# Half of the MLP's gating moved from VectorE to GpSimd, and every engine's order written anew

## The chip, the cores and the metric

The kernel runs on one core of a Trainium2 chip. The metric is the device time of one execution in microseconds (us); the times here are medians of several executions. The engines are PE (TensorE), DVE (VectorE), ACT (ScalarE), POOL (GpSimd) and SP (SyncE, which here only issues DMAs). Each runs its own queue of instructions strictly in order and waits on semaphores for the others.

## The reference, cut to what matters

The program is a transformer block followed by a cross-attention layer, on 4 batches of 1024 rows and 256 channels, all in float32. Four stages follow each other for each row:

```
A  h = LN(x)*(1+s)+b;  x += gate * windowed_self_attention(h)     # windows of 128, 16 heads
B  h = LN(x)*(1+s)+b;  x += gate * topk_cross_attention(h, ctx)   # the 16 largest of 77 scores
C  h = LN(x)*(1+s)+b;  u = h @ w_m1 + b_m1                        # 256 -> 2 x 1024
   a, b = u[..., :1024], u[..., 1024:]
   x += gate * ((silu(a) * b) @ w_m2 + b_m2)                      # 1024 -> 256
D  h = LN(x)*scale+bias;  out = x + cross_attention(h, ctx) @ Wp + bp
```

The change concerns `silu(a) * b` in stage C.

## The kernel before, in words

The 4096 rows are 32 tiles of 128 rows. Every tile passes the four stages, and different tiles are in different stages at the same time: while tile t is normalised for stage A, tile t-1 or so is in B, tile t-4 in C, tile t-6 in D. Each engine has a list of steps (`fill`, then `body(i)` for i = 8 to 31, then `drain`), written out in full: a step such as `up(t, j)` is a few instructions behind its waits. `run(step, i, lag, ...)` in a body calls the step for tile i - lag. The order within these lists is the whole schedule; nothing is chosen while the kernel runs.

PSUM has eight banks of 512 words. Banks 0 to 3 hold the wide score matrices of A, B and D in turn; banks 4 to 7 are shared by all other results, as the table `BANK` says (A's output and the up group 2 are both in bank 5, for instance). `claim` makes PE wait until the last holder of a bank has been read.

Stage C works on the transposed normalised tile `HT["C"]`. The hidden width 1024 is eight groups of 128, one to a partition. For group j, `up(t, j)` (L2336) makes four float32 matmuls, recorded as eight, into bank `C.up{j}`: columns 0 to 127 are a, columns 128 to 255 are b. `silu(t, j)` (L1039, ACT) writes silu(a + bias) to `SA`, and `hidden(t, j)` (L1666, DVE) writes (b + bias) * SA to `G`, of which there are two copies, and frees the bank. `down(t, half)` (L2348, PE) multiplies four groups of `G` with `w_m2` into bank `C.dn0`; half 0 takes groups 0 to 3, half 1 groups 4 to 7. `gated` (DVE) and `add_residual` (POOL) then make the input of stage D.

In `body`, PE's order around this is: transpose_h D, three transpose_p B, scores_t, up 0, project_q D, weigh_values B and A, scores D, up 1, project_o B, up 2 to 4, project_o A, up 5 to 7, down 0, project_k, down 1, project_q A, transpose_h C and B, weigh_values D, scores_a, project_q B, project_o D, project_v, transpose_max, scores B. `maxima_a` (L1522, DVE) reads the scores of scores_a, and transpose_max (L2250) turns what it wrote.

DVE also does the selection of the 16 largest scores (`select`, four units of four heads, steps 0 to 3: MAX8, MATCH_REPLACE8, MAX8, MATCH_REPLACE8), `keep_chosen` (L1583), the statistics of the layer norms, residual adds and transposes. POOL does the reciprocal roots of the norms (`reciprocal_root`, L613), subtractions of maxima (`less_max`, `top_less_max`), normalisations, bias adds and `add_residual` (L703). SP's order places the DMAs: turning the tile and the stage-D weights through DRAM, loads of x and of weights, stores of the output.

Of the kernel before, what the change touches and what calls it, by code (L numbers as in the profile page):

```python
# [7 lines left out]
ALU = mybir.AluOpType  # L8
# [4 lines left out]
P = 128  # L13
# [62 lines left out]
G_COPIES = 2  # L76
TURNED = {"A": range(1, 32)}
WEIGHTS_TURNED = {"D": range(1, 26)}

def block_kernel(nc, a, out):  # L80
    ctx = ExitStack()
    with ctx:
# [87 lines left out]
        with ExitStack() as early:  # L170
# [43 lines left out]
        ld = {n: sem(f"ld_{n}") for n in ("cond", "small", "mod_a", "mod", "gate", "rows", "qkv", "so",  # L214
                                          "b", "kv_b", "kv_d", "up", "down", "ctx")}
# [33 lines left out]
        u_ps, sa_ok, g_ok = sem("u_ps"), sem("sa_ok"), sem("g_ok")  # L249
# [90 lines left out]
        def _(sp):  # L340
# [110 lines left out]
            def fill():  # L451
                write_tables()
                write_turned(1, "A")
                read_tables(0)
                read_turned(1, "A")
                load_next_x(2)
                read_tables(1)
                load_next_x(3)
                write_turned(2, "A")
                read_turned(2, "A")  # L460
                load_context_weights()
                load_mlp_weights(0)
                write_turned(3, "A")
                load_next_x(4)
                read_tables(2)
                read_turned(3, "A")
                write_flat("B")
                load_mlp_weights(1)
                read_flat("B")
                write_turned(4, "A")  # L470
                load_next_x(5)
                read_turned(4, "A")
                load_mlp_weights(2)
                load_next_x(6)
                write_flat("D")
                write_turned(5, "A")
                read_turned(5, "A")
                read_flat("D")
                write_turned(6, "A")
                load_next_x(7)  # L480
                read_turned(6, "A")

            def body(i):
                run(write_weights, i, 8, "D", 0)
                run(write_weights, i, 8, "D", 1)
                run(load_next_x, i, 0)
                run(store_y, i, 9)
                run(read_weights, i, 8, "D", 0)
                run(read_weights, i, 8, "D", 1)
                run(write_turned, i, 1, "A")  # L490
                run(read_turned, i, 1, "A")

            def drain():
                store_y(TILES - 9)
                write_weights(TILES - 8, "D", 0)
                write_weights(TILES - 8, "D", 1)
                read_weights(TILES - 8, "D", 0)
                read_weights(TILES - 8, "D", 1)
                write_turned(TILES - 1, "A")
                read_turned(TILES - 1, "A")  # L500
                write_weights(TILES - 7, "D", 0)
                write_weights(TILES - 7, "D", 1)
                read_weights(TILES - 7, "D", 0)
                read_weights(TILES - 7, "D", 1)
                store_y(TILES - 8)
# [17 lines left out]
            load_weights(rows[:], a["rows"].partition_broadcast(BATCH).rearrange("p a n c -> p (a n) c"), "rows")  # L523
# [6 lines left out]
            load_weights(w_kv["B"][:], a["w_kv"], "kv_b")  # L530
# [12 lines left out]
        def _(pool):  # L543
# [38 lines left out]
            def set_up_value_masks():  # L582
                pool.wait_ge(ld["ctx"], 16 * 3)
# [118 lines left out]

            def add_residual(t):  # L703
# [9 lines left out]
            def fill():  # L713
                reciprocal_root(0, "A")
                reciprocal_root(1, "A")
                set_up_masks()
                add_bias(0, "A")
                add_bias(1, "A")
                set_up_value_masks()
# [3 lines left out]
                set_up_context_rstd()  # L723
                reciprocal_root(0, "B")
                add_bias(2, "A")
                reciprocal_root(3, "A")
                add_bias(0, "B")
                less_max(0, "B", 0)
                divide_a(1)
                add_bias(1, "B")  # L730
                less_max(0, "B", 1)
                reciprocal_root(4, "A")
                reciprocal_root(1, "B")
                top_less_max(0)
                normalise_weights(0, "B", 0)
                add_bias(3, "A")
                normalise_weights(0, "B", 1)
                set_up_values("B")
                less_max(1, "B", 0)
                divide_a(2)  # L740
                top_less_max(1)
                less_max(1, "B", 1)
                reciprocal_root(2, "B")
                reciprocal_root(0, "C")
                normalise_weights(1, "B", 0)
                normalise_weights(1, "B", 1)
                reciprocal_root(5, "A")
                less_max(2, "B", 0)
                add_bias(4, "A")
                less_max(2, "B", 1)  # L750
                add_bias(0, "C")
                divide_a(3)
                set_up_keys("D")
                reciprocal_root(3, "B")
                reciprocal_root(1, "C")
                top_less_max(2)
                add_residual(0)
                normalise_weights(2, "B", 0)
                normalise_weights(2, "B", 1)
                reciprocal_root(0, "D")  # L760
                set_up_values("D")
                clear_pads()
                less_max(3, "B", 0)
                divide_a(4)
                add_bias(1, "C")
                reciprocal_root(6, "A")
                add_bias(2, "B")
                less_max(0, "D", 0)
                top_less_max(3)
                less_max(3, "B", 1)  # L770
                less_max(0, "D", 1)
                add_bias(5, "A")
                reciprocal_root(4, "B")
                add_bias(2, "C")
                reciprocal_root(2, "C")
                add_residual(1)
                normalise_weights(3, "B", 0)
# [3 lines left out]
                add_bias(3, "B")  # L781
                fold_sums(0)
                normalise_weights(0, "D", 0)
                less_max(4, "B", 0)
                divide_a(5)
                reciprocal_root(7, "A")
                normalise_weights(0, "D", 1)
                less_max(1, "D", 0)
                add_bias(1, "D")
                reciprocal_root(3, "C")  # L790
                reciprocal_root(5, "B")
                add_bias(6, "A")
                less_max(1, "D", 1)
                top_less_max(4)
                less_max(4, "B", 1)
                add_residual(2)
                add_bias(7, "A")
                reciprocal_root(2, "D")
                add_bias(4, "B")

            def body(i):
                run(normalise_weights, i, 4, "B", 0)
                run(normalise_weights, i, 4, "B", 1)
                run(fold_sums, i, 7)
                run(reciprocal_root, i, 0, "A")
                run(less_max, i, 3, "B", 0)
                run(add_bias, i, 5, "C")
                run(add_bias, i, 6, "D")
                run(normalise_weights, i, 7, "D", 0)
                run(divide_a, i, 2)  # L810
                run(normalise_weights, i, 7, "D", 1)
                run(less_max, i, 3, "B", 1)
                run(less_max, i, 6, "D", 0)
                run(reciprocal_root, i, 4, "C")
                run(reciprocal_root, i, 2, "B")
                run(add_bias, i, 0, "A")
                run(less_max, i, 6, "D", 1)
                run(top_less_max, i, 3)
                run(add_bias, i, 3, "B")
                run(add_residual, i, 5)  # L820
                run(reciprocal_root, i, 5, "D")

            def drain():
                normalise_weights(TILES - 4, "B", 0)
                normalise_weights(TILES - 4, "B", 1)
                fold_sums(TILES - 7)
                add_bias(TILES - 3, "B")
                normalise_weights(TILES - 7, "D", 0)
                add_bias(TILES - 6, "D")
                divide_a(TILES - 2)  # L830
                add_bias(TILES - 5, "C")
                normalise_weights(TILES - 7, "D", 1)
                reciprocal_root(TILES - 4, "C")
                less_max(TILES - 3, "B", 0)
                reciprocal_root(TILES - 2, "B")
                add_bias(TILES - 4, "C")
                less_max(TILES - 3, "B", 1)
                top_less_max(TILES - 3)
                less_max(TILES - 6, "D", 0)
                less_max(TILES - 6, "D", 1)  # L840
                add_residual(TILES - 5)
# [3 lines left out]
                fold_sums(TILES - 6)  # L845
                less_max(TILES - 2, "B", 0)
                add_bias(TILES - 5, "D")
                less_max(TILES - 2, "B", 1)
                add_bias(TILES - 2, "B")
                normalise_weights(TILES - 6, "D", 0)  # L850
                divide_a(TILES - 1)
                normalise_weights(TILES - 6, "D", 1)
# [55 lines left out]
        def _(act):  # L908
# [1835 lines left out]
```

## Time and profile before

| | us |
|---|---|
| median of 3 runs | 971.22 (970.75 to 972.36) |
| profiled execution | 972.71 |
| its span, first to last instruction | 970.9 |

| engine | busy us | share | instructions |
|---|---|---|---|
| PE | 922.6 | 95% | 10500 |
| DVE | 867.8 | 89% | 4318 |
| ACT | 744.8 | 77% | 1604 |
| POOL | 701.7 | 72% | 1099 |

The profile is one execution, recorded instruction by instruction. A busy share counts the time in which an engine has an instruction in it, and neighbouring instructions overlap: the next one starts before the last has left. So what an instruction costs its engine is better read from one start to the next than from its duration. A releaser is what ended an idle time.

### The profile page before, as it was taken

Reading aid. Unit: us, or ns where it says so; the run is one execution under the profiler, and the core shown is the slowest. Engines: PE = TensorE matmul, PEld = TensorE weight load, DVE = VectorE, ACT = ScalarE, POOL = GpSimd, SP = SyncE. Lnnn points to the kernel's source line nnn. Section 1 sums busy time; section 2 is a strip of 40 time slices with the busy share of each in tenths; the row PEclk is TensorE's granted clock in tenths of the full one; section 3 lists DMA queues with packets and bytes.
Section 4 is the critical chain, followed back from the end, with each engine's and each line's share of the span. In section 5 each row is a group of like instructions: output and inputs, shape, how many; then the busy total and the mean of one; then the engine's idle time right before and its main releaser. Section 6 shows DMA issues by size and latency. Waiting matters only on the chain. (4 is left out here: it accounts for less than half of the span.)

```text
span 970.9 us, 32585 instructions
## 1 busy us (share of the span) xinstructions
PE 922.6 (95%) x10500; PEld 803.2 (83%) x10500; DVE 867.8 (89%) x4318; ACT 744.8 (77%) x1604; POOL 701.7 (72%) x1099
## 2 busy tenths in 40 slices
PE   6777999999999999999999999999999999999996
PEld 4555888888889888888889888888889888888784
DVE  3587999999999999999999999999999999998643
ACT  2464778888878888888888887888888888887773
POOL 1525587887777888887777777887777887777652
PEclk9997999999999999999999999999999999999999
DMA  8464310123333333223333333223333332220000
GB/s 296 139 132 109 37 17 10 31 65 78 72 72 78 78 65 57 62 64 78 72 72 79 77 54 65 62 67 78 72 73 78 78 67 52 50 63 7 7 6 18
DMA packets 210555, 66.44 MB, mean 68 GB/s; under 512 B 188520, under 2 KB 200961, under 8 KB 209746
## 3 DMA queue, kind: packets, MB, share of 16 engines
q1 hardware_dynamic: 210386, 64.35, 30.2%
q8 instruction: 86, 1.41, 0.6%
q14 instruction: 83, 0.68, 0.2%
HBM read 39.02 MB, written 25.30 MB: 66 GB/s over the span
## 5 line engine op out<-in xcount | busy, mean ns | idle before, releaser
L2344 PE MATMUL ps<-hT_C,w_m_sb 128*128 128x128 f32 x2048 | 257.4, 278 | 1.3 <-DVE hidden_C L1674 0.8
L2344 PEld LDWEIGHTS ps<-hT_C,w_m_sb 128*128 128x128 f32 x2048 | 243.8, 192 | 14.5 <-issue 8.3
L1043 ACT ACTIVATE silu_C<-ps,cols_sb 128x128 f32<-128x128 f32 x256 | 93.4, 366 | 117.3 <-PE ps L2344 106.3
L2355 PE MATMUL ps<-w_m_sb,hidden_C 128*128 128x256 f32 x512 | 120.8, 380 | 0.0
L1580 DVE MATCH_REPLACE8 scores_left_B<-mx_B,scores_left_B 128x77 f32<-128x77 f32 x512 | 108.9, 229 | 0.0
L1576 DVE MATCH_REPLACE8 scores_left_B<-mx_B,scores_B 128x77 f32<-128x77 f32 x512 | 108.4, 226 | 0.0
L2355 PEld LDWEIGHTS ps<-w_m_sb,hidden_C 128*128 128x128 f32 x512 | 92.7, 190 | 10.3 <-DVE hidden_C L1674 0.2
L666 POOL TENSOR_TENSOR scores_D<-scores_D,mx_D 128x616 f32<-128x616 f32 x62 | 75.9, 1227 | 25.2 <-DVE mx_D L1647 25.2
L1674 DVE SCALAR_TENSOR_TENSOR hidden_C<-ps,cols_sb,silu_C 128x128 f32<-128x128 f32 x256 | 84.1, 339 | 8.8 <-ACT silu_C L1043 8.7
L701 POOL TENSOR_TENSOR p_B<-p_B,rc_B 128x616 f32<-128x616 f32 x64 | 76.9, 1218 | 17.4 <-DVE p_B L1588 13.0
L701 POOL TENSOR_TENSOR p_D<-scores_D,rc_D 128x616 f32<-128x616 f32 x63 | 77.0, 1225 | 12.0 <-DVE rc_D L1625 6.3
L661 POOL TENSOR_TENSOR p_B<-scores_B,mx_B 128x616 f32<-128x616 f32 x64 | 78.5, 1227 | 8.9 <-DVE mx_B L1574 8.9
L1574 DVE MAX8 mx_B<-scores_B 128x8 f32<-128x77 f32 x512 | 80.1, 227 | 2.6 <-ACT scores_B L1014 2.2
L1578 DVE MAX8 mx_B<-scores_left_B 128x8 f32<-128x77 f32 x512 | 81.4, 225 | 0.0
L1528 DVE TENSOR_REDUCE mx_A<-ps 128x8 f32<-128x1024 f32 x64 | 75.1, 1216 | 3.1 <-PE ps L2246 3.1
L992 ACT ACTIVATE pT_A<-ps 128x1024 f32<-128x1024 f32 x64 | 63.7, 1068 | 2.5 <-PE ps L2263 2.1
L1588 DVE SCALAR_TENSOR_TENSOR p_B<-scores_left_B,p_B 128x616 f32<-128x616 f32 x64 | 51.2, 800 | 1.1 <-ACT p_B L1020 1.1
L976 ACT ACTIVATE kblk_A<-ps,kb_bias,mask_sb 128x128 f32<-128x128 f32 x128 | 47.6, 450 | 3.8 <-PE ps L2226 3.8
L2301 PE MATMUL ps<-ident_sb,p_B 128*128 128x128 f32 x320 | 44.9, 279 | 5.2 <-POOL p_B L701 4.3
L1036 ACT COPY pT_B<-ps 128x512 f32<-128x512 f32 (+1 forms) x96 | 47.7, 540 | 1.6 <-PE ps L2301 1.5
L1647 DVE TENSOR_REDUCE mx_D<-scores_D 128x8 f32<-128x616 f32 x62 | 47.8, 773 | 0.4 <-ACT scores_D L1014 0.4
L1014 ACT COPY scores_B<-ps 128x616 f32<-128x616 f32 x64 | 40.1, 679 | 9.5 <-PE ps L2287 9.1
(188 smaller groups left out, 2434.8 us busy)
## 6 DMA issues: line engine op xcount, KB each, us to landing
p_turned_D<-p_blocks_D SPq DMA_DIRECT2D x200, 80.0 KB, 2.4
pT_D<-p_turned_D SPq DMA_DIRECT2D x50, 320.0 KB, 3.6
xn_turned_A<-xn_blocks_A SPq DMA_DIRECT2D x124, 32.0 KB, 2.0
xn_A<-xn_turned_A SPq DMA_DIRECT2D x31, 128.0 KB, 2.1
x_A<-in_x SPq DMA_DIRECT2D x28, 128.0 KB, 2.3
out<-y_D SPq DMA_DIRECT2D x28, 128.0 KB, 2.0
w_m_sb<-in_w_m SPq DMA_DIRECT2D x3, 1024.0 KB, 5.2
w_mod_sb<-in_w_mod SPq DMA_DIRECT2D x2, 1024.0 KB, 10.0
```

Of the source, the lines that this page charges most:

```text
L661: g.tensor_tensor(where, S["B"][:, heads, :], MXB[:, heads, 0:1].to_broadcast([P, HH, LC]), ALU.subtract).then_inc(sm_ok["B"], 1)
L666: g.tensor_tensor(where, where, MXD[:, heads, :].to_broadcast([P, HH, LC]), ALU.subtract).then_inc(sm_ok["D"], 1)
L701: g.tensor_tensor(where, src, rc, ALU.mult).then_inc(n_ok[s], 1)
L1043: sc.activation(SA[:, j, :], bank(f"C.up{j}")[:, 0:P], ACT.Silu, bias=col("bm1_a", j)).then_inc(sa_ok, 1)
L1528: v.tensor_reduce(MXA[:, :, :, c], wide[:, :, c * 2 * P:(c + 1) * 2 * P].rearrange("p g (j k) -> p g j k", j=2), AX.X, ALU.max).then_inc(m ...
L1574: ins = v.max(MXB[:, h, 0:8], S["B"][:, h, :])
L1576: ins = v.match_replace(R[:, h, :], MXB[:, h, 0:8], S["B"][:, h, :], LOW)
L1578: ins = v.max(MXB[:, h, 8:16], R[:, h, :])
L1580: ins = v.match_replace(R[:, h, :], MXB[:, h, 8:16], R[:, h, :], LOW)
L1674: v.scalar_tensor_tensor(out=G[:, t % G_COPIES, j, :], in0=bank(f"C.up{j}")[:, P:2 * P], scalar=col("bm1_b", j), in1=SA[:, j, :], op0=ALU. ...
L2344: ins = mm(bank(f"C.up{j}")[:, half * P:(half + 1) * P], w_m1[:, k, m:m + P], HT["C"][:, t % HT_COPIES["C"], k, :], start=(k == 0), stop=( ...
L2355: ins = mm(bank("C.dn0")[:, 0:CH], G[:, t % G_COPIES, j, :], w_m2[:, j, :], start=(j == 0), stop=(j == HJ - 1))
```

## The change

`DIRECT = HJ // 2` is 4. Groups 0 to 3 are gated by DVE as before. For groups 4 to 7 `silu` also copies b + bias from the bank into `G` on ACT, which frees the bank, and one POOL instruction a tile multiplies `SA` into `G` in place.

```diff
+DIRECT = HJ // 2
+            def multiply_rest(t):                       # POOL
+                pool.wait_ge(sa_ok, HJ * t + HJ)
+                pool.wait_ge(ub_ok, (HJ - DIRECT) * (t + 1))
+                rest = G[:, t % G_COPIES, DIRECT:, :]
+                g.tensor_tensor(rest, SA[:, DIRECT:, :], rest, ALU.mult).then_inc(gp_ok, 1)
             def silu(t, j):                             # ACT
                 act.wait_ge(u_ps, HJ * t + j + 1)
                 if not first(t):
-                    act.wait_ge(g_ok, HJ * (t - 1) + j + 1)
+                    if j < DIRECT:
+                        act.wait_ge(g_ok, DIRECT * (t - 1) + j + 1)
+                    else:
+                        act.wait_ge(gp_ok, t)
                 sc.activation(SA[:, j, :], bank(f"C.up{j}")[:, 0:P], ACT.Silu, bias=col("bm1_a", j)).then_inc(sa_ok, 1)
+                if j >= DIRECT:
...
+                    if t >= G_COPIES:
+                        act.wait_ge(y_ps["C"], t + 1 - G_COPIES)
+                    sc.activation(G[:, t % G_COPIES, j, :], bank(f"C.up{j}")[:, P:2 * P], ACT.Identity, bias=col("bm1_b", j)).then_inc(ub_ok, 1)
             def up(t, j):                               # PE
-                claim(BANK[f"C.up{j}"], (g_ok, HJ * t + j + 1))
+                if j < DIRECT:
+                    claim(BANK[f"C.up{j}"], (g_ok, DIRECT * t + j + 1))
+                else:
+                    claim(BANK[f"C.up{j}"], (ub_ok, (HJ - DIRECT) * t + j - DIRECT + 1))
             def down(t, half):                          # PE
-                pe.wait_ge(g_ok, HJ * t + (half + 1) * HJ // 2)
+                if half == 0:
+                    pe.wait_ge(g_ok, DIRECT * (t + 1))
+                else:
+                    pe.wait_ge(gp_ok, t + 1)
```

Two semaphores of the fill are merged into others (`rows` into `gate`, `kv_b` into `ctx`), since two new ones are needed. All lists are made anew, steady body, fill and drain, on PE, DVE, ACT, POOL and SP. The steady bodies, where they differ (steps named with their lag):

```diff
 PE    ... weigh_values_a, scores D, up 1,
-      project_o B, up 2, up 3, up 4, project_o A, up 5, up 6, up 7, down 0, project_k, down 1,
-      project_q A, transpose_h C, transpose_h B, weigh_values D, scores_a, project_q B, project_o D, project_v,
+      up 2, up 3, project_o B, project_o A, up 4, up 5, up 6, up 7, down 0, project_k, project_q A, down 1,
+      transpose_h B, scores_a, weigh_values D, project_q B, transpose_h C, project_v, project_o D,
       transpose_max, scores B
 POOL
+      fold_sums 7, normalise D 7 (0, 1), root A 0, divide_a 2, less_max B 3 (0), add_bias D 7, add_bias B 4,
+      less_max B 3 (1), add_bias A 0, add_bias C 5, less_max D 6 (0), top_less_max 3, root B 2,
+      multiply_rest 5, less_max D 6 (1), root C 4, add_residual 5, normalise B 3 (0), root D 5, normalise B 3 (1)
 ACT
+      output_t B, silu 0, modulate A, silu 1 to 3, normalise A, copy_scores D (0, 1), silu 4 to 7,
+      exponentials B (0), normalise B, key_blocks, queries A, top_exponentials, modulate B, normalise C,
+      exponentials B (1), output_t D, exponentials D (0), queries B, modulate C, normalise D, values,
+      exponentials D (1), copy_scores B (0, 1), weights_t B (0, 1, 2), modulate D, exponentials_a (0, 1), queries D
 SP
-      write_weights 0, 1, load x, store y, read_weights 0, 1, write_turned, read_turned
+      read_turned, write_weights 0, 1, read_weights 1, store y, read_weights 0, write_turned, load x
```

On DVE the four remaining `hidden` steps stand after the output turns of stage A, each beside selection steps; `maxima_a` follows `gated`, turn_input, row_sums B and statistics D, and the second keep_chosen now comes after it. In the fill, SP's `load_mlp_weights(1)` and `(2)` move behind `write_flat("D")`, `read_flat("D")` and `read_tables(2)`; PE makes `project_k(0)`, the gates and the bias before `project_q(0, "A")`.

## Rows read from the trace of the kernel before

**Rows 1.** The page's busy time: engine, busy us, share of the span, instructions.
```profile
PE 922.6 (95%) x10500; PEld 803.2 (83%) x10500; DVE 867.8 (89%) x4318; ACT 744.8 (77%) x1604; POOL 701.7 (72%) x1099
```

**Rows 2.** Windows: stretch, length, busy of PE PEld DVE ACT POOL, clock, DMA.
```profile
0.00:100.00 100.00, 71.81 (x636) 53.33 (x636) 63.07 (x283) 44.41 (x96) 37.85 (x89) 0.95 0.59 164
...
200.00:850.00 650.00, 647.55 (x7661) 571.86 (x7660) 631.73 (x3170) 537.40 (x1168) 513.06 (x780) 1.00 0.32 68
850.00:971.00 121.00, 106.04 (x1106) 91.55 (x1105) 79.02 (x366) 82.53 (x171) 73.68 (x102) 0.99 0.08 20
```

**Rows 3.** Timeline, POOL, residual add of tiles 3 and 25: start, us, instruction.
```profile
201.85 0.75 POOL L711 TENSOR_TENSOR x_D<-xg_C,tmp_C 128x256 f32<-128x256 f32 x1
...
802.62 0.73 POOL L711 TENSOR_TENSOR x_D<-xg_C,tmp_C 128x256 f32<-128x256 f32 x1
```

**Rows 4.** Waits, 200 to 850 us: who waits for whom, total us, times, longest.
```profile
PEld ps L2253 <- DVE mx_A L1528: 9.8, 24, 0.5
...
DVE hidden_C L1674 <- ACT silu_C L1043: 1.2, 3, 0.5
...
ACT silu_C L1043 <- PE ps L2344: 80.3, 121, 1.4
...
POOL top_B L674 <- DVE mx_B L1578: 18.1, 23, 1.1
```

**Rows 5.** Timeline of PE, one steady tile.
```profile
506.22 1.03 PE L2236 MATMUL ps<-w_qkv_sb,hT_A 128*128 128x256 f32 x4
507.27 0.33 PE L2253 MATMUL ps<-ident_sb,mx_A 128*128 128x128 f32 x1
...
510.91 1.16 PE L2344 MATMUL ps<-hT_C,w_m_sb 128*128 128x128 f32 x8
511.90 1.06 PE L2215 MATMUL ps<-hT_D,w_qd_sb 128*128 128x128 f32 x8
...
516.50 1.03 PE L2333 MATMUL ps<-w_out_B,oT_B 128*128 128x256 f32 x4
517.37 2.84 PE L2344 MATMUL ps<-hT_C,w_m_sb 128*128 128x128 f32 x24
520.12 1.10 PE L2333 MATMUL ps<-w_out_A,oT_A 128*128 128x256 f32 x4
521.06 2.84 PE L2344 MATMUL ps<-hT_C,w_m_sb 128*128 128x128 f32 x24
523.74 1.89 PE L2355 MATMUL ps<-w_m_sb,hidden_C 128*128 128x256 f32 x8
525.47 1.05 PE L2226 MATMUL ps<-hT_A,w_qkv_sb 128*128 128x128 f32 x8
526.36 1.89 PE L2355 MATMUL ps<-w_m_sb,hidden_C 128*128 128x256 f32 x8
```

**Rows 6.** Page groups of silu and hidden; timelines of DVE and ACT.
```profile
L1043 ACT ACTIVATE silu_C<-ps,cols_sb 128x128 f32<-128x128 f32 x256 | 93.4, 366 | 117.3 <-PE ps L2344 106.3
...
L1674 DVE SCALAR_TENSOR_TENSOR hidden_C<-ps,cols_sb,silu_C 128x128 f32<-128x128 f32 x256 | 84.1, 339 | 8.8 <-ACT silu_C L1043 8.7
...
519.64 0.59 DVE L1674 SCALAR_TENSOR_TENSOR hidden_C<-ps,cols_sb,silu_C 128x128 f32<-128x128 f32 x2
...
502.27 0.60 ACT L964 ACTIVATE qT_A<-ps,cols_sb 128x128 f32<-128x128 f32 x2
```

**Rows 7.** Groups by line and form, POOL adds of two full operands.
```profile
L681 POOL TENSOR_TENSOR fold_D<-scores_D 128x640 f32<-128x640 f32 x30 | 46.6, 1555 | 0.0
...
L684 POOL TENSOR_TENSOR fold_D<-fold_D 128x320 f32<-128x320 f32 x30 | 26.1, 870 | 2.4
```

**Rows 8.** Timelines of DVE and POOL around one keep_chosen.
```profile
504.15 0.80 DVE L1588 SCALAR_TENSOR_TENSOR p_B<-scores_left_B,p_B 128x616 f32<-128x616 f32 x1
...
504.28 0.72 POOL L617 TENSOR_TENSOR ve_D<-mv_D,eps 128x1 f32<-128x1 f32 x1 [1.35 <-DVE mv_D L1501]
504.96 0.19 POOL L618 TENSOR_TENSOR ve_D<-mv_D,neg_one 128x1 f32<-128x1 f32 x1
```

More of the change, by code:

```diff
@@ L828, in drain @@
[L828 to L838, printed above, removed]
@@ L1774, in fill @@
                 select(2, 3, 0)
-                select(2, 2, 0)
-                select(2, 1, 1)
+                hidden(0, 0)
+                residual(1, "B")
+                hidden(0, 1)
+                turn_back(3)
+                select(2, 2, 2)
+                hidden(0, 2)
+                statistics(1, "C")
+                hidden(0, 3)
+                select(2, 0, 2)
                 select(2, 3, 1)
+                residual(3, "A")
+                statistics(3, "B")
                 select(2, 1, 2)
-                select(2, 0, 1)
@@ new lines, in fill @@
+                select(3, 3, 0)
+                select(3, 0, 2)
+                select(3, 1, 2)
+                select(3, 3, 1)
+                turn_outputs(4)
+                select(3, 2, 0)
+                statistics(6, "A")
+                hidden(1, 0)
+                residual(2, "B")
+                select(3, 2, 1)
+                hidden(1, 1)
+                turn_back(4)
+                hidden(1, 2)
+                select(3, 2, 2)
+                hidden(1, 3)
+                select(3, 3, 2)
@@ L1844, in fill @@
+                select(3, 1, 3)
+                residual(4, "A")
+                select(3, 0, 3)
+                statistics(4, "B")
+                select(3, 3, 3)
+                statistics(2, "C")
+                maxima_d(0, 0)
+                select(3, 2, 3)
+                maxima_d(0, 1)
+                keep_chosen(3, 0)
+                gated(1)
+                keep_chosen(3, 1)
                 row_sums(3, "B")
-                gated(1)
-                select(3, 0, 3)
                 statistics(1, "D")
-                keep_chosen(3, 0)
@@ new lines, in body @@
+                run(hidden, i, 6, 0)
+                run(turn_weights, i, 8, "D", 1)
+                run(hidden, i, 6, 1)
+                run(select, i, 4, 1, 2)
+                run(turn_back, i, 3)
+                run(hidden, i, 6, 2)
+                run(select, i, 4, 2, 1)
+                run(select, i, 4, 0, 2)
+                run(hidden, i, 6, 3)
+                run(residual, i, 3, "A")
+                run(residual, i, 5, "B")
+                run(maxima_d, i, 7, 0)
+                run(select, i, 4, 3, 2)
@@ L1930, in drain @@
-                hidden(TILES - 6, 6)
-                hidden(TILES - 6, 7)
+                residual(TILES - 5, "B")
                 statistics(TILES - 3, "B")
+                select(TILES - 4, 3, 2)
+                select(TILES - 4, 1, 2)
                 maxima_d(TILES - 7, 1)
-                select(TILES - 4, 3, 2)
+                turn_input(TILES - 1, "A")
+                select(TILES - 4, 0, 3)
+                select(TILES - 4, 3, 3)
+                statistics(TILES - 5, "C")
                 select(TILES - 4, 1, 3)
-                select(TILES - 4, 2, 3)
+                keep_chosen(TILES - 4, 0)
@@ new lines, in drain @@
+                hidden(TILES - 5, 1)
+                hidden(TILES - 5, 2)
+                turn_back(TILES - 2)
+                turn_weights(TILES - 7, "D", 1)
+                residual(TILES - 4, "B")
+                hidden(TILES - 5, 3)
+                select(TILES - 3, 3, 0)
+                statistics(TILES - 4, "C")
+                select(TILES - 3, 3, 1)
+                select(TILES - 3, 0, 3)
+                select(TILES - 3, 3, 2)
+                residual(TILES - 2, "A")
+                statistics(TILES - 2, "B")
@@ L2563, in body @@
                 run(project_k, i, 0)
+                run(project_q, i, 0, "A")
                 run(down, i, 4, 1)
-                run(project_q, i, 0, "A")
+                run(transpose_h, i, 1, "B")
+                run(scores_a, i, 0)
+                run(weigh_values, i, 6, "D")
+                run(project_q, i, 1, "B")
                 run(transpose_h, i, 3, "C")
-                run(transpose_h, i, 1, "B")
-                run(weigh_values, i, 6, "D")
-                run(scores_a, i, 0)
-                run(project_q, i, 1, "B")
+                run(project_v, i, 0)
                 run(project_o, i, 6, "D")
-                run(project_v, i, 0)
                 run(transpose_max, i, 0)
```

922 lines of the change are left out of this document (427 added, 495 removed).

## The prediction

> **What bounds the kernel now.** I read the busy shares of the page first [rows 1]: PE 95%, DVE 89%, ACT 77%, POOL 72%. These are means over a fill, a steady loop and a drain, so the stretches come next [rows 2]. Between 200 and 850 us PE is busy 647.6 of 650 us and DVE 631.7, while in the first 100 us neither is above 72. The steady loop is where the time lies: the residual add of tile 3 starts at 201.85 and that of tile 25 at 802.62 [rows 3], so one tile takes 600.77 / 22 = 27.31 us. Then the waits of that loop [rows 4]. DVE's only wait for hidden activations there is 1.2 us in 24 tiles: DVE has no idle time, its queue is full. ACT stands 80.3 us waiting for the up projections and POOL 18.1 us for the third selection step alone, so both have room. PE waits for DVE: 9.8 us of weight loads for the maxima, 24 times. Last, one tile on PE [rows 5], where the reader takes each block's length from its start to the next start. Without a wait a block of eight 128x128 matmuls takes 0.89 us (project_k, 525.47 to 526.36), three take 2.68 (up 5 to 7, 521.06 to 523.74), one of four 128x256 matmuls 0.87 (516.50 to 517.37). So two things are nearly full: DVE sets the pace, and PE stands just behind it. How far behind decides this case.
>
> **PE's own need.** In [rows 5] these blocks are longer than their unhindered length: project_v 1.05 against 0.87 (0.18 or 0.19, waiting with the transpose behind it for DVE's maxima), up 2 to 4 with 2.75 against 2.68 (0.07) and project_o of stage A with 0.94 against 0.87 (0.07, its PSUM bank 5 is that of up 2, which hidden 2 frees). That is 0.33; a few hundredths more of the same kind I estimate at 0.03. I leave the rest in: up 0 takes 0.99 (510.91 to 511.90), 0.10 more than 0.89, and it comes right behind scores that use 32 rows of the array, when nothing is late. I take this 0.10 to belong to the change of shape. PE would then need 27.31 - 0.36 = 26.95 us a tile.
>
> **The change, part by part.**
>
> DVE loses four of the eight gating operations of a tile. Two in a row take 0.59 us, one 0.34 on average [rows 6], so each holds DVE for 0.25: 4 x 0.25 = 1.0 us less of 27.31. DVE would need 26.3 and is then no longer the last; it has 0.65 us a tile to wait with.
>
> ACT writes b + bias for column groups 4 to 7 from PSUM into the hidden tile: four 128x128 Identity activations. The query writes are the same form; two take 0.60 us and a silu 0.37 [rows 6], so one holds ACT some 0.25, four 1.0 us a tile. Bounds: 0 (all in idle time) and 4 x 0.37 = 1.5. PE makes an up block each 0.89 us, ACT needs 0.25 + 0.25 for it, and the wait of 80.3 / 24 = 3.3 us a tile lies in just this phase. I take 1.0, all hidden. With Identity next to Silu no table load is added that the orders show.
>
> POOL multiplies 128x512 by 128x512, once a tile. No such row is in the trace. The nearest with two full operands are fold_D with 320 elements, 0.87, and 640, 1.56 [rows 7]; in between 512 gives 0.87 + 192/320 x 0.69 = 1.28 us. Bounds: the two rows themselves, 0.87 and 1.56. POOL is busy 513.1 of 650, that is 21.6 us a tile; with 1.3 it has 22.9 of 26.95. Not a bound by its sum.
>
> Against this speaks the Trainium skill, "GPSIMD Engine Reference", Engine selection: elementwise work belongs on VectorE, GpSimd being about twice as slow on two inputs. The prices agree in direction: DVE 1.0 us for the four, POOL 1.28. Read alone the rule would keep the work on DVE and the time at 971; the rows say DVE is full and POOL isn't.
>
> The wait that is added: the second half of down now waits for POOL's product. Behind it on PE stand transpose_h B, scores_a, and with them ACT and DVE. The chain behind up 7 is silu 0.37, bias write 0.35, product 1.28, with overlaps and signals about 2.0 us. PE's new order puts down 0 (1.73, 523.74 to 525.47), project_k and project_q (0.89 each) between up 7 and down 1: 3.5 us. Slack 1.5 us, if POOL is free. Ahead of the product in POOL's queue are top_less_max, which waits for the third selection step, and the reciprocal root for B, which waits for DVE's statistics. By laying the new orders along [rows 5] at 26.95 us, the root ends about when ACT's last bias write does, and the product ends some 1.2 us before down 1 wants it. Behind the product wait less_max D (half 1) and the residual add; both have over 1 us.
>
> One more risk for this: a 128x1 add on POOL takes 0.72 us when it starts at 504.28, inside keep_chosen on DVE (504.15 to 504.95), and 0.19 just after [rows 8]. Two engines get in each other's way here. The product doesn't lie beside keep_chosen in the new order; if it does, it costs up to 0.8, within the slack. (The Trainium skill, "SBUF — State Buffer", Who interferes with whom, has GpSimd and VectorE on one port pair that one of them holds alone; by that rule, too, the product is late by one DVE operation at most and the sum is the same.)
>
> The moves in the steady order. scores_a goes ahead of weigh_values D, and transpose_h C, project_v and project_o D come between it and transpose_max: about 1.2 us more for DVE's maxima than before, so the 0.19 goes. project_o A comes directly behind project_o B, with DVE's output turns and hidden 2 done some 0.7 us earlier by my layout: 2 x 0.07 goes. Tight places that stay: ACT's query write before scores_a (0.3), POOL's second normalisation of B before its transposes (0.5). Banks of groups 4 to 7 are now freed by ACT within 0.7 us of the matmul; DVE took longer. SP reads back the D weights half 1 first, behind earlier writes; DVE turns them about 2 us sooner and PE wants them 0.7 later, so nothing is late.
>
> Fill and drain are made anew. Before 100 us nothing is full, and PEclk is 0.95 there [rows 2], that is 10 us at the lower level of 1.2 GHz. No row says whether the new fill is better. Bounds: -5 (the lower clock goes, half of 10 us) and +8 (the second MLP load now queues behind the flat writes and reads of D on SP; its distance from up 0 may go). I take 0. In the last 121 us PE is busy 106.0 and DVE 79.0, so DVE's relief is worth little, and the last tile's down 1 comes 0 to 0.5 later. I take 0 there.
>
> **The sum.** Steady stretch 160 to 822 us, 24 tiles x 0.36 = 8.6 us. Seven more tiles in fill and drain with DVE relieved, at the same 0.36: 2.5. Profiled execution 972.7 (span 970.9 and 1.8 around it) - 11.1 = 961.6. It lies 1.5 above the median of 971.22, so the forecast for the median is 960.1, say **960.0**. Own range 954 to 966: 0.23 to 0.50 a tile over 31 tiles, and the ends.
>
> **Rivals.**
> 1. PE's stretched blocks are DVE's shadow too, 0.10 at each of some six shape changes. Then PE needs 26.4, DVE 26.3, and 31 x 0.9 = 28 us at most go, with friction 18 to 25: 946 to 953. For it: DVE was full. Against: up 0 is 0.99 again and again with nothing late.
> 2. The orders give it back: PE is a wall at 27.2 and a new tight place (ACT before scores_a, 0.3 us of slack) takes what the maxima gave. 31 x 0.1 = 3 us or less, and a worse fill: 966 to 973. For it: two engines within 2% of each other, each with small waits. Against: the slacks above.
> 3. Slower: the product comes late. If statistics of B or the third selection step reach POOL 2.5 us later than I lay them, the slack of 1.5 is gone by 1.0 and down 1 stalls PE by 1.0 us each tile, with no 0.36 regained for lack of an earlier scores_a: 24 x (1.0 - 0.36) = +15, and up to +24: 986 to 995. It decides from 1.5 us of lateness on. For it: POOL runs one queue in order and already waits 18.1 / 23 = 0.79 us for DVE at top_less_max in each tile [rows 4]. Against: DVE has 0.65 a tile more room and the selections come earlier in its queue.
>
> **How the numbers follow.** Forecast 0.62; rival 1 0.11; rival 2 0.14, half of it within 0.2%; rival 3 0.13. Within 0.2% is 1.9 us, about what a measurement of this kernel can tell: 969.3 to 973.2. Faster 0.62 + 0.11 + 0.07 = 0.80, same 0.07, slower 0.13. The range of 8 in 10 takes the forecast, most of rival 1 and most of rival 2: 950 to 972.
>
> **What the changed profile would show.** The residual add's period 26.95 us (26.8 to 27.1). DVE with waits for hidden or the down matmul, 0.5 us a tile. project_v at 0.87 and project_o A at 0.87, up 0 still at 0.99 (0.89: rival 1). A POOL product of 1.28 us, x32, and a PE wait for it at the down matmuls near zero (about 1 us per tile: rival 3). Silu's wait for PE down from 3.3 to about 2.3 us a tile. I am wrong if the period stays above 27.2, or if the first residual add moves by more than 5 us from where it is.

## The result, and the profile after

The changed kernel takes 955.27 us (median of 4 runs, 954.34 to 955.88) against 971.62 of the kernel before on the same chip (970.75 to 972.36). The two medians divide to 0.983; the ratio on record, worked out from the single runs, is 0.9825 with a 95% interval of 0.9804 to 0.9845. Forecast was 960.0, range 950 to 972. The sign, the mechanism of the steady loop and the range held; the gain is 16.3 us where I had 11.2, and 5.1 us of what the profiles gained lie in the fill, for which I had taken 0.

Its profiled execution took 954.87 us, span 953.1. The page's busy time, answering [rows 1], and the windows, answering [rows 2] (stretch, length, busy of PE PEld DVE ACT POOL, clock, DMA):

```profile
PE 910.1 (95%) x10500; PEld 798.5 (84%) x10500; DVE 838.6 (88%) x4190; ACT 780.1 (82%) x1732; POOL 730.4 (77%) x1131
```

```profile
0.00:100.00 100.00, 73.86 (x706) 55.37 (x710) 69.33 (x328) 49.23 (x103) 43.60 (x98) 0.98 0.64 170
200.00:850.00 650.00, 649.16 (x7770) 580.00 (x7769) 622.01 (x3140) 573.93 (x1280) 538.82 (x814) 1.00 0.33 70
850.00:953.00 103.00, 88.28 (x919) 75.03 (x917) 56.43 (x258) 70.86 (x155) 69.17 (x90) 0.99 0.03 9
```

PE's share of the whole span has not moved, 95% both times. What moved is the steady stretch: PE is now busy 649.2 of 650 us there, against 647.6, but it gets through 7770 recorded matmuls in place of 7661, 1.4% more. Most of the waiting that went stood inside time that the page calls busy, so block lengths show it and the busy share doesn't. Where the 17.8 us of span went is read from the residual adds x_D, this time of tiles 0, 3, 25 and 31 (timeline of POOL, answering [rows 3]; "tile 0" means the first of these rows):

```profile
115.38 0.72 POOL L719 TENSOR_TENSOR x_D<-xg_C,tmp_C 128x256 f32<-128x256 f32 x1 [2.44 <-DVE tmp_C L1711]
195.49 0.73 POOL L719 TENSOR_TENSOR x_D<-xg_C,tmp_C 128x256 f32<-128x256 f32 x1
786.00 0.73 POOL L719 TENSOR_TENSOR x_D<-xg_C,tmp_C 128x256 f32<-128x256 f32 x1
931.27 0.72 POOL L719 TENSOR_TENSOR x_D<-xg_C,tmp_C 128x256 f32<-128x256 f32 x1 [0.62 <-DVE tmp_C L1711]
```

| stretch | before | after | gain |
|---|---|---|---|
| start to tile 0 | 120.46 | 115.38 | 5.1 |
| tile 0 to 3 | 81.39 | 80.11 | 1.3 |
| tile 3 to 25 (22 periods) | 600.77 | 590.51 | 10.3 |
| tile 25 to 31 | 145.71 | 145.27 | 0.4 |
| tile 31 to the end | 22.6 | 21.8 | 0.8 |

The period is 590.51 / 22 = 26.84 us, from 27.31. Waits from 200 to 850 us, answering [rows 4] (who waits for whom, total us, times, longest):

```profile
ACT silu_C L1063 <- PE ps L2337: 59.7, 143, 2.3
...
DVE tmp_C L1711 <- PE ps L2351: 6.0, 20, 0.7
...
POOL hidden_C L709 <- ACT hidden_C L1071: 0.4, 1, 0.4
...
POOL top_B L676 <- DVE mx_B L1606: 0.6, 1, 0.6
```

PE's weight loads no longer wait for the maxima at all; VectorE has turned from the one waited for into one that waits: 0.3 us for the down projection in 20 of the tiles, and 11.5 us with all its other waits in this stretch, 0.5 a tile as forecast, against 2.7 before. One tile on PE, answering [rows 5], and the end of the product on POOL and of the bias writes on ACT in the same tile:

```profile
508.10 3.73 PE L2337 MATMUL ps<-hT_C,w_m_sb 128*128 128x128 f32 x32
511.67 1.89 PE L2351 MATMUL ps<-w_m_sb,hidden_C 128*128 128x256 f32 x8
513.40 1.05 PE L2216 MATMUL ps<-hT_A,w_qkv_sb 128*128 128x128 f32 x8
514.29 1.06 PE L2205 MATMUL ps<-hT_A,w_qkv_sb 128*128 128x128 f32 x8
515.18 1.89 PE L2351 MATMUL ps<-w_m_sb,hidden_C 128*128 128x256 f32 x8
...
520.52 1.03 PE L2226 MATMUL ps<-w_qkv_sb,hT_A 128*128 128x256 f32 x4
521.39 1.03 PE L2323 MATMUL ps<-w_pd_sb,oT_D 128*128 128x256 f32 x4
...
525.82 1.16 PE L2337 MATMUL ps<-hT_C,w_m_sb 128*128 128x128 f32 x8
526.82 1.06 PE L2205 MATMUL ps<-hT_D,w_qd_sb 128*128 128x128 f32 x8
```

```profile
512.13 0.36 ACT L1071 ACTIVATE hidden_C<-ps,cols_sb 128x128 f32<-128x128 f32 x1
```

```profile
512.20 0.19 POOL L619 TENSOR_TENSOR ve_B<-mv_B,eps 128x1 f32<-128x1 f32 x1
...
513.38 1.28 POOL L709 TENSOR_TENSOR hidden_C<-silu_C,hidden_C 128x512 f32<-128x512 f32 x1
```

Project_v takes 520.52 to 521.39 = 0.87, where it took 1.05. Up 0 still takes 525.82 to 526.82 = 1.00. The product takes 1.28 us and ends at 514.66, 0.5 us before the down half that wants it (its weight load comes a little ahead of the matmul, so 0.4).

### The profile page after: what moved, and what is told of

Its sections match the earlier page's. It is cut to its first block, busy times and chain, and to the rows that moved or that the text cites. A ratio compares the mean times of both kernels' runs of the same rounds, so it can differ in the third digit from the quotient of the medians.

```text
span 953.1 us, 32530 instructions
## 1 busy us (share of the span) xinstructions
PE 910.1 (95%) x10500; PEld 798.5 (84%) x10500; DVE 838.6 (88%) x4190; ACT 780.1 (82%) x1732; POOL 730.4 (77%) x1131
## 4 chain that ended last, share of the span: by engine, by line
PE 85%; DVE 6%; issue 4%; ACT 2%; DMA 1%; POOL 1%; SPq 1%; POOLq 0%; DVEq 0%; ACTq 0%
PE ps L2337 24%; PE ps L2351 10%; PE ps L2205 9%; PE ps L2323 8%; PE ps L2312 6%; PE ps L2277 5%; PE ps L2291 4%; PE ps L2253 4%; PE ps L2236 3%; PE ps L2266 3%; PE ps L2216 3%; PE ps L2226 3%; PE ps L2194 2%; DVE scores_left_B L1604 1%; DVE mx_B L1606 1%
## 5 line engine op out<-in xcount | busy, mean ns | idle before, releaser
L2337 PE MATMUL ps<-hT_C,w_m_sb 128*128 128x128 f32 x2048 | 252.2, 278 | 0.8 <-DVE hidden_C L1702 0.5
L2337 PEld LDWEIGHTS ps<-hT_C,w_m_sb 128*128 128x128 f32 x2048 | 240.0, 192 | 11.5 <-issue 6.7
L1063 ACT ACTIVATE silu_C<-ps,cols_sb 128x128 f32<-128x128 f32 x256 | 93.4, 367 | 77.1 <-PE ps L2337 76.5
L663 POOL TENSOR_TENSOR p_B<-scores_B,mx_B 128x616 f32<-128x616 f32 x64 | 78.5, 1228 | 16.3 <-DVE mx_B L1602 10.9
L1602 DVE MAX8 mx_B<-scores_B 128x8 f32<-128x77 f32 x512 | 75.8, 225 | 6.0 <-ACT scores_B L1031 5.6
L1037 ACT ACTIVATE p_B<-p_B 128x616 f32<-128x616 f32 x64 | 45.5, 715 | 4.7 <-POOL p_B L663 4.4
L683 POOL TENSOR_TENSOR fold_D<-scores_D 128x640 f32<-128x640 f32 x30 | 46.7, 1555 | 0.6 <-ACT scores_D L1037 0.6
L1037 ACT ACTIVATE scores_D<-scores_D 128x616 f32<-128x616 f32 x64 | 47.1, 739 | 0.0
L1071 ACT ACTIVATE hidden_C<-ps,cols_sb 128x128 f32<-128x128 f32 x128 | 46.5, 363 | 0.0
```

What stands on the lines that cost most here:

```text
L663: g.tensor_tensor(where, S["B"][:, heads, :], MXB[:, heads, 0:1].to_broadcast([P, HH, LC]), ALU.subtract).then_inc(sm_ok["B"], 1)
L1037: sc.activation(where, where, ACT.Exp, scale=SCALE).then_inc(e_ok[s], 1)
L1063: sc.activation(SA[:, j, :], bank(f"C.up{j}")[:, 0:P], ACT.Silu, bias=col("bm1_a", j)).then_inc(sa_ok, 1)
L2337: ins = mm(bank(f"C.up{j}")[:, half * P:(half + 1) * P], w_m1[:, k, m:m + P], HT["C"][:, t % HT_COPIES["C"], k, :], start=(k == 0), stop=( ...
```

## The experiments

Periods are means of the 22 from tile 3 to tile 25, read as above; "tile 0" is when the first x_D starts. Ratios are to the kernel before on the same chip.

**1. The orders without the split.** The changed kernel's orders on all engines, all eight groups gated by VectorE, groups 4 to 7 put between the instructions that follow group 3. The steady part of the edit:

```
 run(residual, i, 5, "B")
+run(hidden, i, 6, 4)
 run(maxima_d, i, 7, 0)
+run(hidden, i, 6, 5)
 ...
 run(select, i, 4, 2, 2)
+run(hidden, i, 6, 6)
 ...
 run(maxima_d, i, 7, 1)
+run(hidden, i, 6, 7)
```

> The changed kernel's orders on every engine, but VectorE gates all eight groups of every tile; ScalarE's four Identity passes and GpSimd's product are gone. Theory (VectorE was the bound of the steady tiles, TensorE is now): VectorE gets 8 x .25 = 2.0 us less .. no: 4 x .25 = 1.0 us a tile back on 26.3, so the period is again 27.2 (27.1 to 27.5) and the run takes 24 to 31 x .36, some 8 to 11 us more than the changed kernel: 963 to 967. The stretch to the first tile's residual add of block D is told apart by the same run: if the 5.1 us gained there (120.5 to 115.4) come from the new first iterations, it stays near 115.5; if they come from the split, it goes back to 120. Rival (the new orders alone made the gain, the split is idle): period 26.8 to 26.9, run 954 to 957.

Measured: 989.02 us, ratio 1.019 (1.017 to 1.021). Tile 0 at 115.51, period 27.85. The 5.1 us before tile 0 belong to the new first iterations, as expected: 5.0 of them are there with VectorE gating everything. In the steady loop the orders alone gain nothing and lose 0.5 a tile. The size was off: I expected 27.2, and a run of 963 to 967. VectorE waits 0.5 us a tile for silu in this run (11.6 us, 24 times), which depends on where I happened to put groups 4 to 7; without that wait VectorE would be back at about 27.3, as before (an estimate: 27.85 - 0.5). The 27.85 is thus no verdict on the best all-VectorE form of these orders.

**2. The split without the orders.** The kernel before with its own orders; groups 4 to 7 over ACT and POOL, and nothing else but the wait counters that this needs.

```
 run(reciprocal_root, i, 2, "B")
+run(multiply_rest, i, 5)
 run(add_bias, i, 0, "A")
 run(less_max, i, 6, "D", 1)
 run(top_less_max, i, 3)
```

> The kernel before with its own orders; only groups 4 to 7 go over ScalarE's Identity and GpSimd's product, which stands behind the reciprocal root of block B in the steady order. Theory: the period falls to 26.85 to 27.0 because VectorE lost 1.0 us a tile, the first residual add of block D stays at 120 (the fill gain belongs to the new first iterations), run 962 to 966. Rival (the orders made the gain): period 27.2, run 970 to 973. Rival (the split made all of it, fill too): 955 to 958, first residual add near 115.5.

Measured: 990.00 us, ratio 1.020 (1.018 to 1.022). Tile 0 at 126.17, period 27.29. The theory fell here: VectorE lost its four operations, and the period did not follow. The 19.7 us by which this run's span is longer all lie outside the steady loop: 5.7 before tile 0, 2.0 from there to tile 3 and 12.3 after tile 25, in first and last iterations that were never laid out for the product (the merged load counters, which this kernel has too, were not tried apart). Inside the loop, the chain of waits in one steady tile (start, us, what; "issue" is time for which the profile names no wait) shows the new bound:

```profile
504.99 1.27 POOL hidden_C L721
...
506.91 0.10 POOL scores_D L678
...
507.10 1.58 issue
508.68 0.61 POOL top_B L686
...
509.64 0.29 ACT xn_A L967
...
510.13 0.60 ACT qT_A L993 x2
510.73 0.15 ACT p_B L1049
510.89 0.35 issue
511.24 0.81 ACT hT_B L982 x2
```

and POOL's timeline beside it:

```profile
504.99 1.27 POOL L721 TENSOR_TENSOR hidden_C<-silu_C,hidden_C 128x512 f32<-128x512 f32 x1
506.22 0.73 POOL L657 TENSOR_TENSOR xg_A<-x_A,gate_b 128x256 f32<-128x256 f32 x1
506.91 1.80 POOL L678 TENSOR_TENSOR scores_D<-scores_D,mx_D 128x616 f32<-128x616 f32 x1
508.68 0.60 POOL L686 TENSOR_TENSOR top_B<-mx_B 128x256 f32<-128x256 f32 x1
```

The 1.58 of "issue" is filled by POOL's 128x616 subtraction. VectorE's last third-step selection ended at 506.65, top_B started at 508.68: product, bias add and a subtraction stood ahead of it in POOL's queue, and ACT and PE follow top_B. The operation that left one engine's critical queue had entered another's.

**3. VectorE lighter, before and after.** Both kernels leave out the second replacement for one head of four in each unit of the selection, 0.82 us of VectorE a tile:

```
-for h in range(u * HU, (u + 1) * HU):
+for h in range(u * HU, (u + 1) * HU - (step == 3)):
```

> The kernel before, leaving out the second replacement of the top-k selection for one head of four in each unit (four MATCH_REPLACE8 of .2 us less a tile, .82 us of VectorE). Theory (VectorE bounds the steady tiles of before down to TensorE's own need of 26.84): period 26.85 to 26.95, run 958 to 964. Rival (TensorE's or the order's cost, not VectorE's work, set 27.24): period 27.2, run 969 to 972.

> The changed kernel with the same cut of .82 us a tile on VectorE. Theory (TensorE is the bound, with 26.84 of work and no wait): period 26.84 unchanged, run 953 to 956. Rival of the prediction (the .10 us at up 0 is VectorE's shadow, and VectorE still bounds): period 26.4 to 26.7, run 943 to 951.

Measured: before 963.12 us, ratio 0.992 (0.990 to 0.994), period 26.98, its median 26.88; after 955.32, ratio 0.984 (0.982 to 0.985), period 26.83, against 26.84. Taking work from VectorE gains 0.33 a tile before and nothing after. That VectorE was the bound and is so no longer is shown, and rival 1 of the prediction is out: VectorE's shadow does not reach below 26.84. (What was left out is also a link of the selection's chain; this run alone doesn't tell VectorE's load from that chain, but its waits in the kernel before, 2.7 us in 650, leave it hardly any idle time.)

**4. PE lighter, before and after.** Both kernels leave out one of the eight down matmuls of a tile (two of its recorded passes):

```
-for j in range(half * HJ // 2, (half + 1) * HJ // 2):
+for j in range(half * HJ // 2, (half + 1) * HJ // 2 - half):
```

> The changed kernel, leaving out the last of the eight down-projection matmuls of each tile (.43 us of TensorE a tile). Theory (TensorE is the wall, VectorE has some .5 us a tile left): period 26.84 less .43, 26.4 to 26.5, run 941 to 944. Rival (TensorE and VectorE or the order's loops bind together at 26.84): period 26.7 or more, run 949 to 955.

> The kernel before with the same matmul left out. Theory (VectorE with its order bounds before at 27.24, TensorE has .40 us a tile to spare): period 27.2 unchanged, and only fill and drain gain, run 966 to 970. Rival (TensorE's own work set the pace, its waits are gaps of its queue): period 26.8, run 956 to 959.

Measured: after 947.58, ratio 0.975 (0.973 to 0.977), period 26.60; before 970.76, ratio 0.9984 (0.9973 to 0.9996), period 27.32, unchanged. PE's work sets the changed kernel's pace and not that of the one before. But only 0.24 of the expected 0.43 came back. To find who took the rest, both cuts were made in one kernel:

> The changed kernel with both cuts: one down-projection matmul less a tile (.43 us of TensorE) and one second replacement less in each unit (.82 us of VectorE). The TensorE cut alone gave 26.60, .24 less, not .43. Theory (VectorE itself needs 26.6 a tile in the changed kernel, so it took over at .24): with VectorE lighter the period is TensorE's 26.41 (26.4 to 26.45), run 940 to 943. Rival (the wait of TensorE for ScalarE's queries of block A, .25 a tile in that run, comes from ScalarE's or GpSimd's order): period 26.55 to 26.6, run 945 to 948.

Measured: 947.55, ratio 0.976 (0.973 to 0.978), period 26.59. My theory fell: VectorE is not what stands at 26.6. PE's timeline of that run and its wait in 200 to 850 us show it:

```profile
511.86 1.46 PE L2351 MATMUL ps<-w_m_sb,hidden_C 128*128 128x256 f32 x6
513.22 0.41 PE L2194 MATMUL ps<-ident_sb,xn_B 128*128 128x128 f32 x2
```

```profile
PEld ps L2236 <- ACT qT_A L981: 6.1, 24, 0.3
```

The shortened block takes 1.36 where the whole one takes 1.73, 0.37 less, and the transpose behind it takes 0.42 where it took 0.31, since scores_a waits for ACT's query write. 0.37 - 0.11 = 0.26. That the block shrank by 0.37 and not by 0.43 is a wait too. In the lighter kernel before, where project_q A follows, it does shrink by 0.43:

```profile
525.80 1.46 PE L2355 MATMUL ps<-w_m_sb,hidden_C 128*128 128x256 f32 x6
527.10 1.05 PE L2215 MATMUL ps<-hT_A,w_qkv_sb 128*128 128x128 f32 x8
```

In the changed kernel transpose_h B follows. It goes into bank 6, which project_k filled and ACT's key_blocks must first have read (`claim`). ACT in the run with both cuts:

```profile
511.60 1.48 ACT L993 ACTIVATE kblk_A<-ps,kb_bias,mask_sb 128x128 f32<-128x128 f32 x4
512.96 0.63 ACT L981 ACTIVATE qT_A<-ps,cols_sb 128x128 f32<-128x128 f32 x2
```

The transpose starts 0.14 us after key_blocks' end (513.08 to 513.22), in this tile and at the median of the steady tiles, against 0.50 in the changed kernel; scores_a starts 0.05 after the query write, against 0.30. The view of waits doesn't name the first of the two; that it is the bank is read from the code and these distances. So the next limit behind PE's 26.84 is ACT's run of work from the last bias write to the query write, about 0.25 us away: the query write is the place that the prediction named tight. The cut lies on PE between up 7 and scores_a, beside this run of ACT. What a cut of PE elsewhere in the tile gives back was not tried.

**5. The product late.** The changed kernel with the product behind the second block D subtraction:

```
-run(multiply_rest, i, 5)
 run(less_max, i, 6, "D", 1)
+run(multiply_rest, i, 5)
```

> The changed kernel with GpSimd's product moved behind the second block D subtraction in the steady order, so it ends 1.18 us later. It ended .41 us before the second half of the down projection wanted it. Theory (TensorE has no other work while it waits, so what is late is paid in full): .77 us a tile late, period 27.5 to 27.7, run 971 to 976, slower than before. Rival (the lateness is absorbed, since the subtraction that moves ahead of it comes earlier, or the down half starts later anyway): period 26.84 to 27.0, run 955 to 960.

Measured: 974.43, ratio 1.0025 (1.0011 to 1.0039), period 27.64. PE's timeline of one tile:

```profile
497.16 1.06 PE L2205 MATMUL ps<-hT_A,w_qkv_sb 128*128 128x128 f32 x8
498.73 1.99 PE L2351 MATMUL ps<-w_m_sb,hidden_C 128*128 128x256 f32 x8 [0.52 <-POOL hidden_C L709]
```

0.80 a tile for 0.77 of lateness (1.18 later, less the 0.41 that it had to spare): with PE as the wall, lateness is paid one to one. This is rival 3 of the prediction made real. The 0.47 gained by the rest of the change stays and the lateness comes on top of it, 27.64 against 27.31 before. One line of one queue turns the 1.7% gain into a loss of 0.25%, and in the changed kernel lateness begins to cost after 0.4 us.

**6. Mending the old orders.** If POOL's queue ate the split's gain in experiment 2, moving lines of that queue should bring it back. First top_less_max directly behind the product:

```
 run(multiply_rest, i, 5)
+run(top_less_max, i, 3)
 run(add_bias, i, 0, "A")
 run(less_max, i, 6, "D", 1)
-run(top_less_max, i, 3)
 run(add_bias, i, 3, "B")
 run(add_residual, i, 5)
```

> The split-only kernel (old orders, groups 4 to 7 over ScalarE and GpSimd) with one line of GpSimd's steady order moved: the subtraction of the top maxima of block B goes ahead of the block A bias add and the second block D subtraction, straight behind the product. In the split-only run it began 2.0 us after VectorE had its maxima ready (508.68 against 506.65), because product, bias add and subtraction stood ahead of it on GpSimd, and TensorE then waited for what ScalarE makes of it. Theory (the split's gain was eaten by GpSimd's order, a loop through the top-k): period 26.85 to 27.0 in place of 27.25, run 6 to 9 us under the split-only kernel's 990, 981 to 984. Rival (ScalarE's 1.0 us a tile of Identity passes ate it): period stays at 27.2 or more, run 989 to 991.

Measured: 999.49, ratio 1.028 (1.026 to 1.030), period 27.75. Worse than both sides expected. Its waits, 200 to 850 us:

```profile
DVE st_D L1537 <- POOL x_D L731: 21.7, 23, 1.0
PEld ps L2293 <- DVE mx_A L1568: 17.1, 23, 1.2
POOL top_B L686 <- DVE mx_B L1618: 15.9, 23, 1.0
```

POOL now stands 0.69 a tile at top_B, so everything behind it is later, x_D too; VectorE waits 0.94 for x_D in its own order, and PE for VectorE's maxima. So, with the second block D subtraction (1.23 us) behind the residual add as well:

```
 run(add_residual, i, 5)
+run(less_max, i, 6, "D", 1)
```

> The split-only kernel with the top maxima early (the run before of this line of experiments, period 27.70), and the second block D subtraction (1.23 us) moved from ahead of the residual add x_D to behind it on GpSimd. There VectorE waited .94 us a tile for x_D (statistics of block D), and TensorE .74 + .35 us for VectorE's block A maxima behind it. Theory (GpSimd's in-order stretch from the product to x_D is the loop that eats the split's gain in the old orders; with x_D 1.2 us earlier VectorE's wait is gone): period 26.85 to 27.0, run 970 to 978, since fill and drain of this kernel stay long. Rival (ScalarE's extra 1.0 us a tile, or another loop, holds the old orders at before's pace or above): period 27.2 to 27.7, run 982 to 999.

Measured: 982.85, ratio 1.012 (1.010 to 1.014), period 27.04, median 26.99. VectorE's wait for x_D is gone. Two lines moved on POOL take the old steady order with the split from 27.29 to 27.04, under the 27.31 of before: with POOL's queue laid out for it, the split gives a gain in the old orders too. (The same two lines moved without the split were not tried, so a part of the 0.27 could be theirs.) The run as a whole is slower than before by what lies outside the steady loop, as in experiment 2: tile 0 at 123.89 (before 120.46), and 178.4 us from tile 25 to the end (before 168.3).

**7. The drain.** In the last tiles PE waits for the product: from 846 us on

```profile
PEld ps L2351 <- POOL hidden_C L709: 1.7, 3, 1.1
PE ps L2351 <- POOL hidden_C L709: 0.7, 1, 0.7
```

Tiles 30 and 31 were given back to VectorE whole (direct(t) is the number of groups gated there; their groups 4 to 7 follow group 3 in its last iterations), beside one more run of the changed kernel on the same chip.

```
+def direct(t):
+    return HJ if t >= TILES - 2 else HJ // 2
```

> The changed kernel once more, to stand beside the next one on the same chip: 955 (954 to 957).

> The changed kernel, but the last two tiles (30 and 31) have all eight groups gated by VectorE, which is busy 56 of the last 103 us; the product, which in tiles 28 to 31 ends just when or up to .75 us after TensorE wants it, falls away there. Theory (in the drain the product's 1.3 us lies on TensorE's path): 1 to 2 us less than the changed kernel, 953 to 954.5. Rival (the drain is bound by the chain through block D's attention, whatever gates block C): no difference within 0.2%, 955.

Measured: 955.77 and 955.75. No difference, in the period or from tile 25 to the end (167.5 us both). This doesn't settle what the drain's waits cost, since the edit missed the longest of them: PE's 0.7 and its weight loads' 1.1 are tile 29's and are there as before; what went is 0.2 of tile 31. No version here that does the whole work beats the changed kernel.

## Why the prediction was right, and where it was off

**The steady period: right mechanism, 0.36 sized for 0.47.** The blocks of PE that I took to be stretched are the ones that shrank. Mean start to start, tiles 3 to 25: project_v and the transpose behind it 1.29 to 1.07 (0.22; I had 0.19), project_o of block A 0.94 to 0.86 (0.07 as written), the up projections 7.47 to 7.35 (0.11; I had 0.07), all others together 0.06 (I had 0.03). That is the step of the prediction that the gain rests on, and it held block by block. The rest of the miss is that one tile on the timeline [rows 5] was a typical one: the median period of before is 27.24, and a few of 27.6 lift the mean to 27.31. The changed kernel has almost none of these. 22 x 0.11 = 2.4 us. On the two profiled executions I forecast 11.1 and measured 17.8: 2.4 more in this stretch, 5.1 in the fill, 0.7 less in what remains.

**The 0.10 at up 0: right.** It is 1.00 in the changed kernel, and in every cut of VectorE's work, so it is not VectorE's shadow; that it belongs to the change of shape fits, but no run tests it. In the changed kernel the shortest occurrence of each block of PE in tiles 3 to 25 adds up to 26.82 and the period is 26.84: hardly a block is longer than it must be in this sequence. That is the wall, and 0.82 us less on VectorE does not move it.

**VectorE's 1.0 less, and 26.3: right in effect.** Its time is off the path; that its own need lies below 26.6 follows from experiment 4, since that period didn't move when VectorE got 0.82 lighter. How far below, nothing here shows.

**The product: price right, slack too large.** 1.28 us as worked out from the two rows [rows 7]. But it ends 0.4 us before PE wants it, not 1.2: POOL starts it 0.9 us after ACT's last bias write (513.38 against 512.49), because the reciprocal root of block B stands ahead and is later than I laid it. Rival 3 was closer than I wrote: the product came 0.8 us later than I had laid it, and 0.4 more would have begun to cost. That its cost is what I wrote (1.0 late, 1.0 paid) is what experiment 5 shows. The 0.36 that I wrote would not be regained then is regained all the same, as the lower of my two sums for this rival had it.

**ACT's 1.0 hidden: right.** Silu's wait for PE went from 3.3 to 59.7 / 24 = 2.5 us a tile (I said 2.3), and both traces have 66 table loads. Hidden doesn't mean free of risk: the last bias write stands at the head of the run of ACT that experiment 4 found to be the next limit.

**The Trainium skill's rule.** "GPSIMD Engine Reference", Engine selection, would keep the product on VectorE. Prices of the trace: 1.28 on POOL for 1.0 on VectorE, so the direction agrees. The kernel is 1.7% faster for breaking it, together with its new orders, because the pricier engine had idle time at that place and the cheaper one set the pace; experiment 2 is the same trade with all orders left alone, and there the rule would have been right.

**Rival 2, the orders give it back: wrong for this pair, and a truer warning than I gave it credit for.** The orders without the split, the split in the old orders and its two mended forms are slower than before by 1.2 to 2.8%, and one line moved in the right pair makes it 0.25% slower than before.

**Fill: the term that was mis-sized.** I took 0 with bounds of -5 and +8; it was -5.1, past the edge at which I had called myself wrong. The 5.1 us are thus luck, not forecast. My reason for a possible gain, the lower clock going away, does not carry it. The stretches at 1.2 GHz before tile 0 do shrink, from 10.2 us (76.5 to 80.0, 86.8 to 93.6) to 3.4 (94.7 to 98.1). But among the kernels with the new first iterations tile 0 hardly follows them: the second run of the changed kernel (none of them before tile 0) has it at 114.85, experiment 1 (none) at 115.51, and the changed kernel of experiment 3 (6.8 us of them) at 115.54. The windows 60 to 100 of before, of after and of experiment 1, in this order:

```profile
60.00:100.00 40.00, 28.39 (x250) 20.97 (x250) 31.58 (x181) 21.76 (x51) 19.40 (x38) 0.87 0.56 116
```

```profile
60.00:100.00 40.00, 30.06 (x320) 22.63 (x324) 38.23 (x231) 25.33 (x54) 25.00 (x47) 0.96 0.62 149
```

```profile
60.00:100.00 40.00, 29.32 (x356) 22.26 (x360) 38.22 (x231) 25.88 (x56) 25.00 (x47) 1.00 0.65 148
```

With the new first iterations VectorE is busy 38.2 of 40 us there, with the old ones 31.6. The first up projection starts at 98.4 in place of 104.2, so the gain is there before stage C begins. I had judged the fill by its mean over 100 us (VectorE 63) and found nothing full. The fuller VectorE fits an order that lets it do more early. What the runs show is that the gain comes with the new first iterations and not with the split (experiments 1 and 2); which of the moved lines does it, on which engine or in the loads' order, was not tried.

## What to carry to other kernels

When two engines stand within 2% of each other, moving work off the first gains at most the distance to the second: add up the second one's blocks at their unhindered length, over several tiles and not one, before you move anything. Then follow the moved operation through the queue that it enters, to each instruction that stands behind it; in the changed kernel one line of that queue made the difference between 1.7% faster and 0.25% slower. A kernel written out in full also has first and last iterations: in experiment 2 they cost 20 us where the steady loop cost nothing. Judge a fill by short windows, each on its own.

## What I had not expected

- keep_chosen on VectorE, which I had watched for the product [rows 8], hit others: in experiment 2 it starts at 506.83 and the 128x616 subtraction of POOL at 506.91 takes 1.80 us in place of 1.23; in the first mending of experiment 6 it starts at 508.55 and top_B at 508.63 takes 1.19 in place of 0.60. In experiment 2 it is 0.55 to 0.63 in every tile where the two lie side by side, and in the kernel before 0.3 for top_B: where an operation of POOL lies beside VectorE's is a cost of the order too.
- The changed kernel's median period and its mean agree within 0.01 us, those of before differ by 0.07: with PE as the wall and hardly a wait, one tile takes as long as the next.
